# Two steps of an attention round reordered on TensorE, and the matching copies and splits on ScalarE and VectorE

## The reference

```python
x = x + _L0_xattn_ref(_layernorm(x), ctx_512, Wq, w_kc_q, w_kc_kv, W_qr, W_kr, Wo)
# inside, for hidden_q = layernorm(x) and kv_c = ctx_512:
q_hk = (hidden_q @ Wq.T).reshape(Bv, Sv, H, K)
q_big = jnp.einsum('bshk,hkq->bshq', q_hk, w_kc_q)
q_big = _apply_rope(q_big, sin_q, cos_q)
q_r = jnp.einsum('bshq,hqr->bhsr', q_big, W_qr)
k_r = jnp.einsum('bld,hdr->bhlr', kv_r, W_kr)
attn = softmax(jnp.einsum('bhsr,bhlr->bhsl', q_r, k_r))
ctx_c = jnp.einsum('bhsl,bld->bhsd', attn, kv_r)
ctx_lat = jnp.einsum('bhsd,hkd->bhsk', ctx_c, w_kc_kv)
```

## Time and profile before

| | |
|---|---|
| median of 3 runs | 379.34 us (379.07 to 379.62) |
| profiled execution, own time | 379.05 us |
| its span, first to last instruction | 376.8 us |
| TensorE matmul busy in the span | 362.0 us, 96% |
| VectorE busy | 293.1 us, 78% |
| ScalarE busy | 207.2 us, 55% |
| GpSimd busy | 174.2 us, 46% |
| mean granted TensorE clock | 1.000 |

### The profile page before, as it was taken

One profiled execution on the slowest core, in us unless ns is written; L12 is line 12 of the kernel. 1 busy time (PEld: TensorE's weight loads), 2 busy tenths in 40 slices (PEclk: granted clock), 3 DMA queues, 4 the chain that ended last, 5 costly groups with the idle time before them and its releaser, 6 DMA issues.

```text
span 376.8 us, 6340 instructions
## 1 busy us (share of the span) xinstructions
PE 362.0 (96%) x2193; PEld 269.1 (71%) x2193; DVE 293.1 (78%) x674; ACT 207.2 (55%) x555; POOL 174.2 (46%) x163
## 2 busy tenths in 40 slices
PE   8899999999999999999999999998999999989996
PEld 8775776777677767876767587864557567779885
DVE  5698698698668786986796656578899988896773
ACT  1524576566647664865575495616975371682240
POOL 2453765486458546754765440581711042146000
PEclk9999999999999999999999999999999999999999
DMA  7639100300301203000004000400000000000101
GB/s 230 237 114 336 77 1 2 111 3 1 114 0 17 96 2 112 3 0 2 0 1 155 2 1 0 124 0 1 2 1 2 0 2 1 0 2 2 40 16 56
DMA packets 9086, 17.53 MB, mean 47 GB/s; under 512 B 2144, under 2 KB 6944, under 8 KB 8160
## 3 DMA queue, kind: packets, MB, share of 16 engines
q1 hardware_dynamic: 9056, 17.14, 13.5%
HBM read 16.09 MB, written 1.05 MB: 45 GB/s over the span
## 4 chain that ended last, share of the span: by engine, by line
PE 67%; DVE 14%; POOL 9%; ACT 4%; issue 3%; DMA 2%; SPq 0%; DVEq 0%; POOLq 0%
PE bank L1523 15%; PE bank L1564 8%; PE bank L1582 7%; PE bank L1573 6%; PE bank L1607 4%; PE bank L1548 4%; POOL prob L463 4%; PE bank L1533 3%; PE bank L1476 3%; PE bank L1827 2%; DVE relu L1159 2%; PE bank L1443 2%; DMA blobs<-in_blob 2%; POOL rot_low L458 2%; PE bank L1444 2%
## 5 line engine op out<-in xcount | busy, mean ns | idle before, releaser
L463 POOL TENSOR_TENSOR prob<-prob,rinv 128x512 f32<-128x512 f32 x64 | 66.0, 1042 | 78.4 <-DVE rinv L1023 78.4
L1523 PE MATMUL bank<-xnT,w 128*128 128x512 f32 x288 | 83.1, 425 | 1.7 <-DVE xnT L920 1.7
L621 ACT ACTIVATE prob<-bank,negmax 128x256 f32<-128x256 f32 x128 | 59.7, 488 | 29.5 <-DVE negmax L1017 29.5
L1017 DVE TENSOR_REDUCE negmax<-bank 128x2 f32<-128x512 f32 x64 | 40.9, 681 | 37.7 <-PE bank L1564 37.7
L1523 PEld LDWEIGHTS bank<-xnT,w 128*128 128x128 f32 x288 | 52.4, 188 | 22.0 <-issue 13.3
L631 ACT COPY probT<-bank 128x512 f32<-128x512 f32 x64 | 35.2, 592 | 23.6 <-PE bank L1573 23.6
L951 DVE TENSOR_TENSOR rot_up<-bank,cb 64x512 f32<-64x512 f32 x64 | 44.1, 689 | 1.6
L458 POOL TENSOR_TENSOR rot_low<-rot_low,rot_up 128x512 f32<-128x512 f32 x32 | 41.0, 1282 | 3.8 <-DVE rot_up L951 3.8
L443 POOL TENSOR_TENSOR c_y<-c_ve,minus_half 128x4 f32<-128x4 f32 (+1 forms) x9 | 9.8, 1087 | 57.8 <-DVE c_ve L901 45.5
L1573 PE MATMUL bank<-ca,prob 128*128 128x128 f32 x256 | 34.2, 273 | 0.3 <-POOL prob L463 0.3
L1573 PEld LDWEIGHTS bank<-ca,prob 128*128 128x128 f32 x256 | 30.1, 140 | 5.3 <-POOL prob L463 0.8
(11 more groups left out here) (212 smaller groups left out, 702.7 us busy)
## 6 DMA issues: line engine op xcount, KB each, us to landing
blobs<-in_blob SPq DMA_DIRECT2D x7, 1024.0 KB, 4.8
xs<-in_x SPq DMA_DIRECT2D x2, 512.0 KB, 4.0
xn<-in_w_fc_t SPq DMA_DIRECT2D x1, 1024.0 KB, 4.9
ctxT<-in_w_proj_t SPq DMA_DIRECT2D x1, 1024.0 KB, 5.4
out<-qk SPq DMA_DIRECT2D x8, 128.0 KB, 1.7
cb<-in_const_b SPq DMA_DIRECT2D x1, 768.0 KB, 8.5
blobs<-in_w_gate SPq DMA_DIRECT2D x1, 704.0 KB, 5.7
blobs<-in_w_up SPq DMA_DIRECT2D x1, 704.0 KB, 7.1
```

The source lines that it names most:

```text
L463: pool.tensor_tensor(p[:], p[:], rinv[:, n % PROBS, :].unsqueeze(2).to_broadcast([P, 2, S]), ALU.mult).then_inc(normed, 1)
L621: ins = act.activation(prob[n % PROBS][:, st, :], pS[n % UNITS][:, st * S:(st + 1) * S], ACT.Exp, bias=negmax[:, n % UNITS, st:st + 1], ac ...
L1017: dve.tensor_reduce(negmax[:, n % UNITS, :], pS[n % UNITS][:].rearrange("p (a s) -> p a s", a=2), AX, ALU.max, negate=True).then_inc(max_r ...
L1523: ins = pe.matmul(q_bank(m)[:], w[a][:, k, r * P:(r + 1) * P], x[b][:, k, c * CH:(c + 1) * CH], start=(i == 0), stop=(i == 5))
```

## The change

On TensorE the shared part of u moves from between the first and the second query product of a round to behind the second, and the first fold moves from ahead of the third query product to behind it. On ScalarE the copy of u moves behind the fourth unit's exponentials. On VectorE the split of the folded weights moves from ahead of the third rotation to behind it. This holds in rounds 0 to 13; folds and splits are there in rounds 0 to 11.

```diff
@@ scalar
                 exponentials(n + 2)
+                exponentials(n + 3)
                 u_copy(g + 1)
-                exponentials(n + 3)
                 turned_probs(n)
@@ vector
                 rope_crossed(m + 1, 0)
                 rope_crossed(m + 1, DC)
-                if first is not None:
-                    w1_low(*first)
                 if g == SCALE_ROUND:
...
                 rope(m + 2)
+                if first is not None:
+                    w1_low(*first)
                 if g in LARGEST_ROUNDS:
@@ tensor
                 latent_q(m)
+                latent_q(m + 1)
                 latent_u(g + 1, 1)
-                latent_q(m + 1)
                 turn_probs(n)
                 turn_probs(n + 1)
-                if first is not None:
-                    prep(*first)
                 if g == SCALE_ROUND:
...
                 latent_q(m + 2)
+                if first is not None:
+                    prep(*first)
                 turn_probs(n + 2)
                 turn_probs(n + 3)
                 if second is not None:
                     prep(*second)
```

## The result

The changed kernel takes 390.48 us (median of 6 runs, 389.70 to 393.69) against 379.48 us (6 runs, 379.07 to 380.24): a ratio of 1.0304 over the runs, 95% interval 1.0264 to 1.0345; the quotient of the two medians is 1.029. The forecast was 391.3 us. The profiled execution took 393.69 us, the slowest of the six, with a span of 391.5 us.

A forecast was written before the change was run, and what follows sets the result against it. TensorE's own list was taken to bound the rounds. Six odd-round stalls of 1.83 us (11.0) plus 1.0 in round 0 gave 379.34 + 12.0 = 391.3 us, range 389.5 to 393.5, own range 390.3 to 392.5.

The forecast's parts named there:

- What bounds the kernel: TensorE's own list sets the rounds: busy 12.72 of 12.72 us in round 2, 12.96 of 12.96 in round 3.
- The rival in which slack absorbs it: Another chain times the rounds and the wait disappears: 379.3 us; 3 in 100 for no change, 2 in 100 for faster.
- The split in odd rounds: Second fold waits for the split, now behind the third rotation: 1.83 us in each of six odd rounds, 11.0 us.
- Round 0: Round 1's own u, ahead of its contexts, waits for the late split of round 0: 1.03 us once.
- Even rounds: In round 2 the split ends 0.55 us before the next round's own u loads its weights: no cost.
- Joints and moved products: TensorE's moved u, fold and query products keep their lengths; joints cost 0; earlier query products are hidden.
- The far end of 4.8 us: Four joints at 0.2 us each in six even rounds: 391.3 + 4.8 = 396.1 us, 2 in 100.
- The later u and its copy: Shared u ends 1.39 us later, its copy near 78.2 in round 3, before the next uses: cost 0.
- a lost cover: If the later copy of u were not hidden, fold and scores would wait for 0.6 us of copy.
- The cast: The high weights' cast, near 80.5 to 81.1 in round 3, is not what the split waits for.
- The clock: Rival: stalls drop TensorE to 1.2 GHz until next scores end, doubling 5.5 us seven times: 430 us, 2 in 100.
- The sum: 11.0 us in odd rounds plus 1.0 in round 0, 12.0 us: 391.3 us, own range 390.3 to 392.5.

The follow-up runs named there:

- Putting the contexts first: Changed kernel with round 1 doing its contexts ahead of the own u: 388.85 us, ratio 1.024 to the kernel before; round 0 at 12.26 us.
- split-put-back kernel: Changed kernel with VectorE's edit undone, the split ahead of the third rotation again: 382.76 us, ratio 1.009 to the kernel before.
- u alone: Kernel before with only shared u behind the second query product and its copy behind the fourth exponentials: 380.29 us, ratio 1.0033.
- the copy put back: Changed kernel with ScalarE's edit undone, the copy of u ahead of the fourth exponentials again: 404.58 us in one run.
- two experiments: Changed kernel with the split ahead of the third rotation again, 382.76 us; kernel before with only the first fold moved, 382.75 us (one run).

## Why the prediction was right

**What bounds the kernel.** Right. TensorE's list sets the rounds, and a wait put into it goes through to the end: 11.34 us in the rounds, 11.00 us in the medians. The rival in which slack absorbs it had nothing for it.

**The split in odd rounds.** Right in mechanism, 0.13 us too dear each: 1.83 forecast, 1.70 measured. The rotation and its successor took 86.90 - 84.78 = 2.12 us, as taken. What was off is the start: the third rotation began 84.78 - 76.52 = 8.26 us behind the scores, against 80.11 - 71.74 = 8.37 as read from round 3 before. In the even rounds before, but for round 6, it had been 8.27 there too (67.29 - 59.02 in round 2), so odd rounds of the kernel before had 0.1 us on VectorE that they no longer have. It arises at the round's first reciprocal, 3.09 us behind the scores in round 3 before and 2.97 after; why is open. The wake-up was 0.06 us and not 0.08. Six times 0.13 is 0.8 us.

**Round 0.** Right: 1.03 forecast, 1.12 measured. TensorE resumed at 46.42, 0.15 us behind the split, where I had taken 0.08:

```profile
46.42 1.08 PE L1548 MATMUL bank<-rot_low,wqk 128*64 128x512 f32 x4 [1.56 <-DVE w L913]
```

Putting the contexts first took it away. The split-put-back kernel, at 12.84, shows that it is the split and not the fold.

**Even rounds.** Right: the split of round 2 ends at 74.82 and the own u's weights load at 75.35, 0.53 us later; 0.55 was forecast.

```profile
74.20 0.62 DVE L913 TENSOR_TENSOR w<-bank,w 128x256 fp32r<-128x256 f32 x2
```

```profile
75.35 0.36 PEld L1548 LDWEIGHTS bank<-rot_low,wqk 128*64 128x64 f32 x4
```

**Joints and moved products.** Right for this order: the even round takes 12.71 us against 12.72. The far end of 4.8 us was far off. (What the prediction calls two u matmuls is one fp32 matmul, which the trace shows as two records; its length of 0.86 us is right.) The later u and its copy are hidden. The prediction priced a lost cover at 0.6 us of copy; u alone shows 0.1 us a round where the fold stays in its old place, and the copy put back shows the dearer side, which it did not price: 7 us if ScalarE's order stays as it was.

**The cast.** The prediction said that the cast is not what the split waits for. True with the split behind the rotation. It did not say that the fold's later cast makes the old place of the split bad as well, 4 us as two experiments show. With the fold behind the third query product neither place of the split is free, and the new one is the dearer by 7.4 us.

**The clock.** I gave 2 in 100 to a fall of the clock behind each stall and priced it at 5.5 us. In the changed kernel none of the seven stalls, of 1.45 and 1.56 us idle, lost the clock. Nor did the other seven of 1.43 to 1.55 us, in the two kernels that keep some of them. With 1.97 to 2.30 us idle, 8 of 15 did in three profiles, at 1.6 to 1.7 us each. So the mechanism is real, and the stalls that showed it were some 0.5 us longer than those of the changed kernel. Its price was three times too high, because the clock was back after 3.4 us, where the prediction let it stay low until the next scores end. The Trainium skill, TensorE: Matmul & The Clock Gate, section HAM oscillation, describes such falls behind waits of 3 to 5 us for a transfer. These traces agree on the fall (0.76 against 1.00 over two such stretches), and show it behind waits of 2 us, where equal waits of 1.97 us in one execution went both ways.

**The sum.** 12.0 us forecast, 11.3 measured in the rounds; the time came out 0.8 us below the forecast, inside its own range.

## What to carry to other kernels

Where two steps share one bank or buffer, a move of the first pulls along everything that reads it: follow the chain of fold, cast, split and next fold to its end before moving any of them. Put a short instruction that another engine waits for ahead of a long one that none waits for, and give the waiting engine independent work that stands between. Where a wait of about 2 us on TensorE can't be avoided, look at the granted clock behind it: small matmuls in the wait can be worth more than they cost, as in the one kernel where it was tried.

## What the runs showed of the hardware

- Inside the rounds the granted clock fell behind 8 of 15 TensorE waits of 1.97 to 2.30 us and behind none of 14 of 1.43 to 1.56 us. Outside them it fell once behind a wait of 1.99 us, and in 2 of 12 profiles behind one and the same wait of 0.8 us, so a short wait is no guarantee. A fall cost 1.6 to 1.7 us. Six matmuls of 128 columns in the wait (12 records, 1.50 us) prevented it in all six places.
- The same program loses its clock in some executions and not in others, in stretches that no change touches (0.63 from 268 to 276 us, 0.72 from 8 to 14 us of the changed kernel's profile). That makes 1 to 3 us of scatter in a time of 380 us, more than several of the effects here; rounds of one kind repeat within 0.05 us in a trace where the clock held.
- A weight load that waits for VectorE started 0.06 us behind the end of its last instruction in the second fold, and 0.15 us behind it in the own u. The own u waits for more semaphores; that this makes the difference is not shown.
